# Last pair's cross-attention scores in the projection banks, ahead of and inside the output product of the pair ahead

## What is computed

```python
x = x + rwkv(layernorm(x))
# cross-attention, 16 heads of 32
q, k, v = xn @ Wq.T + bq, ctx @ Wk.T + bk, ctx @ Wv.T + bv
scores = clip(q . k / sqrt(32), -50, 50)      # masked keys: -50
probs = softmax(scores)
delta = 0.05 * ((probs . v) @ Wo.T + bo)
x = x + layernorm(delta) * gamma + beta
# feed-forward, 512 -> 2048 -> 512, ternary weights, 8-bit activations
h = gelu(bitlinear(x, w1, b1))
x = x + bitlinear(h, w2, b2)
```

## Time and profile before

| | before |
|---|---|
| median of 3 runs | 876.15 us (875.24 to 876.9) |
| profiled execution, its own time | 875.0 us |
| span of its instructions | 873.2 us |
| granted TensorE clock, mean | 0.98 |
| TensorE busy | 827.3 us (95%) |
| VectorE busy | 738.1 us (85%) |
| ScalarE busy | 505.0 us (58%) |
| GpSimd busy | 139.1 us (16%) |
| share of the chain that ended last | TensorE 72%, VectorE 16%, issue 5%, GpSimd 4% |

### The profile page before, as it was taken

How to read it: one execution, slowest core, us unless ns; L and a number is a source line. 1 busy time by engine, 2 the same in 40 slices (tenths; PEclk the granted TensorE clock), 3 DMA queues, 4 the chain that set the end, 5 groups by cost and what they waited for, 6 DMA issues and landing times.

```text
span 873.2 us, 23820 instructions
## 1 busy us (share of the span) xinstructions
PE 827.3 (95%) x10117; PEld 666.5 (76%) x10134; DVE 738.1 (85%) x1206; ACT 505.0 (58%) x728; POOL 139.1 (16%) x197
## 2 busy tenths in 40 slices
PE   7898999999999999999889999999999978999997
PEld 6798988888898888889777788888888845444453
DVE  5987989899898989986575689889888979999995
ACT  5566372846546374643535436435444457999995
POOL 1001020100102010100102000000000123676441
PEclk9899999999999999999879999999999989999999
DMA  8330112030211202023140340430232120242311
GB/s 256 126 110 19 44 34 90 15 110 15 69 44 50 75 14 86 15 86 108 65 170 2 146 162 8 146 144 29 115 144 97 39 98 25 87 143 98 109 67 55
DMA packets 36553, 72.41 MB, mean 83 GB/s; under 512 B 6081, under 2 KB 6977, under 8 KB 35433
## 3 DMA queue, kind: packets, MB, share of 16 engines
q1 hardware_dynamic: 35912, 68.93, 23.9%
q0 software_dynamic: 544, 2.10, 0.6%
HBM read 58.39 MB, written 12.58 MB: 81 GB/s over the span
## 4 chain that ended last, share of the span: by engine, by line
PE 72%; DVE 16%; issue 5%; POOL 4%; ACT 1%; DMA 1%; DVEq 0%; POOLq 0%; SPq 0%; ACTq 0%
PE P L62 11%; PE P L63 9%; PE P L64 9%; PE S L750 6%; PE S L2290 5%; PE P L2276 4%; POOL sm L378 3%; DVE xf L1026 3%; DVE E L1862 2%; PE S L636 2%; PE S L1723 2%; PE S L62 2%; PE S L63 2%; PE S L64 2%; PE S L1710 2%
## 5 line engine op out<-in xcount | busy, mean ns | idle before, releaser
L378 POOL TENSOR_TENSOR sm<-sm,mhalf 128x16 f32<-128x16 f32 x8 | 30.6, 3828 | 303.7 <-DVE sm L1121 303.7
L2290 PE MATMUL S<-wq,hqT 128*128 128x512 bf16 x255 | 59.9, 380 | 2.6 <-ACT hqT L2214 2.2
L750 PE MATMUL S<-R,K 64*64 64x32 f32 x3072 | 57.2, 223 | 2.8 <-DVE K L1072 1.7
L750 PEld LDWEIGHTS S<-R,K 64*64 64x64 f32 x3072 | 51.5, 137 | 10.4 <-issue 4.7
L2276 PE MATMUL P<-wq,xqT 128*128 128x512 bf16 x240 | 56.1, 387 | 2.3 <-ACT xqT L2192 1.2
L1862 DVE TENSOR_SCALAR E<-S,upper 128x2048 f32<-128x2048 f32 x16 | 37.6, 2349 | 24.2 <-PE S L1710 24.0
L1536 ACT ACTIVATE E<-E 128x2048 f32<-128x2048 f32 x16 | 30.6, 1913 | 45.3 <-DVE E L1862 45.3
L1868 DVE RECIPROCAL rec<-S 128x512 f32<-128x512 f32 x16 | 53.6, 3350 | 1.8 <-PE S L1725 1.8
L1026 DVE TENSOR_TENSOR xf<-P,xx 128x1024 f32<-128x1024 f32 x40 | 48.7, 1218 | 7.3 <-PE P L657 7.2
L1033 DVE TENSOR_TENSOR xf<-xf,xnT 128x1024 f32<-128x1024 f32 x40 | 49.1, 1227 | 1.1
L2276 PEld LDWEIGHTS P<-wq,xqT 128*128 128x128 bf16 x256 | 24.7, 100 | 29.3 <-issue 2.7
(11 more groups left out here) (300 smaller groups left out, 2701.0 us busy)
## 6 DMA issues: line engine op xcount, KB each, us to landing
wch<-in_wff SPq DMA_DIRECT2D x32, 256.0 KB, 3.1
cwch<-in_wff SPq DMA_DIRECT2D x8, 1024.0 KB, 7.0
xt<-in_x SPq DMA_DIRECT2D x8, 512.0 KB, 4.5
y<-in_x SPq DMA_DIRECT2D x8, 512.0 KB, 3.6
out<-y SPq DMA_DIRECT2D x8, 512.0 KB, 3.3
cxt<-out SPq DMA_DIRECT2D x8, 512.0 KB, 4.1
ct<-in_ctx SPq DMA_DIRECT2D x8, 512.0 KB, 5.1
cxr<-out SPq DMA_DIRECT2D x8, 512.0 KB, 7.0
```

Of the source, the lines that this page charges most:

```text
L378: pool.tensor_tensor(sm[:, 2, :], sm[:, 1, :], mhalf[:, 0:2 * H], ALU.pow).then_inc(y_rstd, 1)
L750: mm = pe.matmul(ps[half_rows(side), par, b, k, :], K[head_rows(par), r % 2, at:at + HALF], right_tokens(par, g, side, i), start=True, sto ...
L2290: mm = pe.matmul(O[:, :], hqT[b % 2][:, k, :], w2q[:, k, :], start=k == 0, stop=k == NF - 1)
```

## The change

The last pair's scores no longer go through `scores` and `clip`. The first set is written to P[2], P[3], S[2] and S[3] before `project_out(6)`, which needs only S[0] and S[1]. The second set is written to the four banks of P between the two halves of `project_out(6)`, as soon as VectorE has clipped the half of the first set that lay in P. VectorE clips the first set in two halves inside its last regular step, ahead of pair 5's `add_last`, and the second set ahead of the feed-forward block's first front. The hand-written lists that follow are reordered on TensorE, ScalarE and VectorE: both `weigh` come before product 0, `project_out(7)` comes before turn 1 and product 1, and ScalarE's `high_out(7)` comes behind GELU 0 and its `center`, VectorE's `low(7)` ahead of front 1. GpSimd's and SyncE's lists stay as they are.

```diff
--- before.py
+++ after.py
@@ -1338,7 +1338,7 @@
     shd = sb("shd", [P, 2])
     shf = sb("shf", [P, 2])
     ident, mhalf = persist["ident"], persist["mhalf"]
-    PFa, PFb, S = psum["X0"], psum["X1"], psum["S"]
+    PFa, PFb, F, S = psum["X0"], psum["X1"], psum["F"], psum["S"]
 
     wload = {n: sem(f"wload_{n}") for n in "qkvo"}
     wsplit_hi = sem("wsplit_hi")
@@ -1357,6 +1357,7 @@
     v_ready = sem("v_ready")
     scores_done = sem("scores_done")
     clipped = sem("clipped")
+    first_clipped = sem("first_clipped")
     exps = sem("exps")
     pv_done = sem("pv_done")
     rec_ready = sem("rec_ready")
@@ -1618,20 +1619,20 @@
         def finish(f):
             last = PAIRS - 1
             run_to_last(act, step)
+            attend(last, 0)
             copy_delta(last - 1)
+            attend(last, 1)
             f["copy_x"](0)
-            attend(last, 0)
-            attend(last, 1)
+            f["gelu"](0)
+            f["center"](0)
+            high_out(last)
+            f["square"](0)
             normalize_delta(last - 1)
-            f["gelu"](0)
             f["copy_x"](1)
-            f["center"](0)
-            f["square"](0)
-            high_out(last)
+            copy_delta(last, d_last)
             f["gelu"](1)
             f["center"](1)
             f["square"](1)
-            copy_delta(last, d_last)
             f["copy_x"](2)
             f["copy_h"](0)
             f["step"](4)
@@ -1682,7 +1683,7 @@
                 mm = pe.matmul(ps, os_[1][:, k, T * b:T * b + T], W["o"][0][:, k, :], start=False, stop=k == NC - 1)
             return mm
 
-        def project_out(r):
+        def project_out(r, between=None):
             if isinstance(r, int) and r == 0:
                 pe.wait_ge(wsplit_lo, 4)
                 pe.wait_ge(bias_lo, 2)
@@ -1693,7 +1694,28 @@
                 if b == 0:
                     pe.wait_ge(ol_ready, r + 1)
                 mm = out_low(S[:, b, :], b)
+                if b == 0 and between is not None:
+                    between()
             mm.then_inc(out_done, 1)
+
+        def score_banks(banks, b):
+            for k in range(NC):
+                for j in range(4):
+                    rows = slice(XD * j, XD * j + XD)
+                    mm = pe.matmul(banks[j][:, T * k:T * k + T], K[rows, k, T * b:T * b + T], Q[rows, k, T * b:T * b + T],
+                                   start=True, stop=True)
+            mm.then_inc(scores_done, 1)
+
+        def last_scores_first():
+            pe.wait_ge(q_ready, NC * PAIRS)
+            pe.wait_ge(k_ready, NC * PAIRS)
+            pe.wait_ge(o_ready, 2 * (PAIRS - 1))
+            score_banks([F[:, 2, :], F[:, 3, :], S[:, 2, :], S[:, 3, :]], 0)
+
+        def last_scores_second():
+            pe.wait_ge(v_ready, PAIRS)
+            pe.wait_ge(first_clipped, 1)
+            score_banks([F[:, j, :] for j in range(4)], 1)
 
         def scores(q, b):
 
@@ -1804,19 +1826,17 @@
         def finish(f):
             last = PAIRS - 1
             run_to_last(pe, step)
-            project_out(last - 1)
-            scores(last, 0)
-            pe.wait_ge(k_ready, NC * PAIRS)
-            pe.wait_ge(v_ready, PAIRS)
+            last_scores_first()
+            project_out(last - 1, last_scores_second)
+            pe.wait_ge(delta, last)
+            weigh(last, 0)
             f["turn_x"](0)
-            scores(last, 1)
+            weigh(last, 1)
             pe.wait_ge(ternary, PAIRS)
             f["product"](0)
-            weigh(last, 0)
-            weigh(last, 1)
+            project_out(last)
             f["turn_x"](1)
             f["product"](1)
-            project_out(last)
             pe.wait_ge(o_ready, 2 * PAIRS)
             f["turn_x"](2)
             pe.wait_ge(delta, PAIRS)
@@ -1861,6 +1881,21 @@
                     dve.wait_ge(pv_done, 2 * q)
             dve.tensor_scalar(E[b][:, :, :, :].rearrange("p j k t -> p (j k t)"), S[:, :, :].rearrange("p j n -> p (j n)"),
                                              upper[:, bass.ds(q * 2 + b, 1)], -LIMIT, ALU.min, ALU.max).then_inc(clipped, 1)
+
+        def clip_last_first():
+            q = PAIRS - 1
+            dve.wait_ge(scores_done, 2 * q + 1)
+            dve.wait_ge(pv_done, 2 * q)
+            dve.tensor_scalar(E[0][:, 0:2, :, :].rearrange("p j k t -> p (j k t)"), F[:, 2:4, :].rearrange("p j n -> p (j n)"),
+                              upper[:, 2 * q:2 * q + 1], -LIMIT, ALU.min, ALU.max).then_inc(first_clipped, 1)
+            dve.tensor_scalar(E[0][:, 2:4, :, :].rearrange("p j k t -> p (j k t)"), S[:, 2:4, :].rearrange("p j n -> p (j n)"),
+                              upper[:, 2 * q:2 * q + 1], -LIMIT, ALU.min, ALU.max).then_inc(clipped, 1)
+
+        def clip_last_second():
+            q = PAIRS - 1
+            dve.wait_ge(scores_done, 2 * q + 2)
+            dve.tensor_scalar(E[1][:, :, :, :].rearrange("p j k t -> p (j k t)"), F[:, :, :].rearrange("p j n -> p (j n)"),
+                              upper[:, 2 * q + 1:2 * q + 2], -LIMIT, ALU.min, ALU.max).then_inc(clipped, 1)
 
         def attended(q, b):
 
@@ -1954,6 +1989,8 @@
                 low(q, os_, o[:, :, :, :].rearrange("p k b t -> p (k b t)"), oh_ready, ol_ready)
                 if first:
                     quantize(1)
+            if isinstance(q, int) and q == PAIRS - 2:
+                clip_last_first()
             if r is not None:
                 add_last(r)
 
@@ -1989,17 +2026,16 @@
             last = PAIRS - 1
             run_to_last(dve, step)
             f["open"]()
+            clip_last_second()
             f["step"](0)
-            clip(last, 0)
+            attended(last, 0)
+            attended(last, 1)
             last_stats(last - 1)
-            clip(last, 1)
+            low(last, os_, o[:, :, :, :].rearrange("p k b t -> p (k b t)"), oh_ready, ol_ready)
             last_norm(last - 1)
             f["step"](1)
-            attended(last, 0)
-            attended(last, 1)
             f["middle_variance"](0)
             f["middle"](0)
-            low(last, os_, o[:, :, :, :].rearrange("p k b t -> p (k b t)"), oh_ready, ol_ready)
             f["middle_scale"](0)
             f["front"](2)
             f["step"](3)
```

## The result

| | before | changed |
|---|---|---|
| median, measured side by side | 875.69 us (4 runs, 874.18 to 876.90) | 885.46 us (4 runs, 884.56 to 886.62) |
| profiled execution, its own time | 875.0 us | 886.62 us |
| span of its instructions | 873.2 us | 884.8 us |
| granted TensorE clock, mean | 0.98 | 0.977 |

The changed kernel takes 1.0113 [1.0091, 1.0135] of the time before. It is **slower by 9.8 us**. The forecast was slower by 6.1.

The account below looks back on a forecast made before the run. The start of the gapless feed-forward steps, the first `xo` at 744.05, was taken to bound the kernel. GELU 1's 7.6 us delay, partly returned, plus a second dip made it 6.1 late: 876.15 + 6.1 = 882.3 us, range 878.8 to 885.7.

Parts of the forecast that it names:

- Steps 1 to 3: Seam start: early scores, clips ahead of the first normalization, then product 0 until 714.6; GELU 0 at 714.7, 1.2 us gained.
- Step 4: Last output product: `coh` at 719.0, TensorE idle 5.5 us, product charged 7.85 us at the dipped clock, ending at 728.0.
- Step 5: Product 1 behind the last output product: starts at 729.5 instead of 719.80, GELU 1 at 733.3, 7.6 us late.
- Step 6: Product 2: starts at 740.8 instead of 735.94, 4.8 us late, 2.8 of the 7.6 being returned.
- Step 7: First VectorE `output` (`xo`): 4.4 us late at full clock, 6.1 us late, at 750.2, with a second clock dip.
- The second dip: Half clock on product 2 after TensorE idles 4.8 us, charged 1.71 us (5.11 against 3.40).
- The 129.15 us behind the first `xo`: Feed-forward steps from the first `xo` to the end, taken as untouched by the change.
- the first dip: Half clock in the last output product after TensorE's 5.5 us idle; charged 7.85 us against 6.12 at full clock.
- longer dips: Rival, 12%: each clock dip lasts 6.8 us instead of 3.4, losing at most 1.7 each; up to 885.7 us.
- faster: Rival, 4%: removing VectorE's waits of 1.65 and 1.60 brings the first `xo` forward by 3.2 us; 872.9 us.
- full clock: Rival, 10%: scores and weighings keep TensorE busy, both dips (1.73 and 1.71) fall away; 878.8 us.
- No difference: Rival, 5%: slack behind takes up the 4 to 6 us, or the rearrangement hides and costs nothing; 876.2 us.

Follow-up runs that it names:

- The second run: The changed kernel with turn 1, product 1 and what feeds them ahead of the last output product again; 882.85 us, ratio 1.0077.
- the first experiment: The changed kernel with its early scores and clips kept, but everything behind them in the order of before on three engines; 878.95 us, ratio 1.0030.
- e2: Same kernel as the second run: the changed kernel with product 1 and its feeding lists ahead of the last output product; 882.85 us, ratio 1.0077.
- e3: The changed kernel with ScalarE making `coh` ahead of GELU 0 instead of behind its centering; 883.15 us, ratio 1.0085.
- e4: The changed kernel with overwritten matmuls filling TensorE's gaps, 22 ahead of the last output product and 24 ahead of product 2; 881.51 us, ratio 1.0074.
- the best lists: The first experiment's kernel with the last clip behind the first normalization, first weighing ahead of product 0, and VectorE's `middle` ahead of `middle_variance`; 874.90 us, ratio 1.0001.

## Why the prediction was right or wrong

**Right:** the side, the chain that makes the time, and its place. Slower had a chance of 0.91. The time, 885.46, is 3.2 us above the forecast and only 0.24 below the top of the range; the repeat, 885.87, lies just above it. That top was worked out for two dips of 6.8 us; the dips were shorter, and the 1.5 us behind the seam, which nothing in the prediction stands for, helped to carry the time up to it. That the number fell inside is partly luck. Of the signs named, GELU 2 at 744 to 746 and the first `xo` at 748 to 750 were missed: by before's time they came at 748.1 and 751.9. Step by step:

- Steps 1 to 3, scores, clips, first product. Product 0 was forecast at +15.35 and came at +15.55, at full clock. A half clip costs half a clip, as I took it. The table load hides behind product 0: ScalarE issued it at 712.45, right behind its last copy, and the GELU began at 717.37, as the product ended. GELU 0 gained 0.82 us, not 1.2. Of a table switch, the Trainium skill (ScalarE: Activation LUTs, What ACT_TABLE_LOAD costs) says that it takes about 1.28 us of load and 1.38 of drain, 2.66 together. The trace agrees with the first figure only. In the kernel before the GELU starts 1.30 us after the load, so no drain of that size is in the path; the measurement decides.
- Step 4, `coh` and the last output product. `coh` came 0.34 late, TensorE's idle time was 5.38 for 5.5. The product's own term was mis-sized: charged 7.85, **measured 8.82**, since it stood at half clock for 5.6 us (722.70 to about 728.3), where the row that set the price did for 3.5.
- Step 5, product 1 behind it. This is the step that costs, as said: GELU 1 is 8.87 us late, forecast 7.6. Of the 1.24 more, 0.97 are step 4's. The step takes it that product 1's operands are there when the output product ends, and never looks. VectorE's list, with `low` and so `coh` ahead of the second normalization, gave them at +30.91, 1.5 us ahead of the forecast turn at +32.45. That it held is luck, and the run with `coh` ahead of GELU 0 shows it failing. The second run and the one with the copy moved bear out the mechanism, with one addition: the sentence that the copy of the last `d` "is hidden behind product 1" holds in the changed kernel but not once product 1 is moved, where it costs 4.7 us at the first `xo`.
- Step 6, product 2: 5.75 us late, forecast 4.8. The excess is that of GELU 1, less 0.3.
- Step 7, first `xo`: 7.83 late, forecast 6.1. The second dip was charged 1.71. Product 2 until its bias took 743.96 to 749.88, 5.92, against 732.82 to 736.36, 3.54, for product 1 at full clock: **2.38**. The price of 1.71 was taken from a product 0 that stood at half clock only from 709.16 to 712.6, 3.4 of its 5.11 us; product 2 did from 743.96 to about 748.8, 4.8 us. The row of a product's 3.40 also holds only 15 of its 16 matmuls; to the bias, all 16 take 3.54.
- The 129.15 us behind the first `xo`, "that the change doesn't touch". This **failed**, by 1.50 us, and it is the term that I had no line for. One interval between two `xo` is 9.28 instead of 8.90. And at the end a wait of about 2 us on TensorE is followed by half clock in one kernel and not in another. TensorE's timeline, first of the changed kernel:

```profile
871.04 5.31 PE L2326 MATMUL S<-wq,hqT 128*128 128x512 bf16 x16 [1.97 <-ACT hqT L2250]
```

Of the kernel before:

```profile
860.81 3.40 PE L2290 MATMUL S<-wq,hqT 128*128 128x512 bf16 x15 [2.20 <-ACT hqT L2214]
```

And of the first experiment:

```profile
864.22 3.63 PE L2327 MATMUL S<-wq,hqT 128*128 128x512 bf16 x16 [1.97 <-ACT hqT L2251]
```

All three are the same product at the same place, the last but one. The changed kernel and the first experiment wait the same 1.97 us; one then runs at half clock and the other at full. The runs with a profile fall into two groups, 130.65 to 130.76 us behind the first `xo` (the change, its repeat, e2, e3, e4) and 129.14 to 129.57 (before and all the others). What sorts them wasn't tested.

The sum, then: 6.1 forecast; 1.0 more for the first dip, 0.7 more for the second, 1.5 behind the seam. That is 9.3, and the medians differ by 9.8. The rival "longer dips" named the right cause for the seam's excess, and its price of up to 1.7 a dip covers both; it was given 12%, and says nothing of the 1.5 us behind the seam. The rival "faster" wanted the last output product to start by about 715 in before's time; it started at 720.4. Whether 715 is the point wasn't tested: with `coh` ahead of GELU 0 it started at 717.05, and the result was slower than before all the same. The rival "full clock" is refuted by the windows. "No difference" fell too, but what stood for it came true by itself: the Trainium skill (TensorE: Matmul & The Clock Gate, HAM oscillation — how this bites in real kernels) reports for another matmul kernel that PSUM double-buffering gave no further gain, and with the lists mended the runs here agree: 874.90 and 876.02 us with the early scores, against 875.36 and 875.83.

## What to carry to other kernels

When a list is rewritten by hand, look at each engine for the first instruction that waits for another engine, and list all that stands behind it. Then ask, for what stands behind, whether its own operands would have been there: here TensorE's product 1 stood behind a product that waited for `coh`, and so did VectorE's normalization that feeds it, so TensorE's list alone shows only part. The next GELU, once product 1 was early, stood behind a copy that waited. Undoing the first order on all its lists gave back 3 of the 10 us, undoing both gave back all. Taking waits away by a buffer was worth little here: the best lists took VectorE's marked waits in the seam from 4.5 to 3.4 us, and no median shows it.

## What was not expected of the hardware

- The same wait of 1.97 us on TensorE, in the same place (the last product but one), was followed by 1.2 GHz in one kernel (5.31 us for 16 matmuls) and by 2.4 GHz in another (3.63). Waits of 2.29 us and 2.07 us were followed by half clock, one of 2.20 us by full. So a dip can't be read off the length of the gap alone. The Trainium skill (TensorE: Matmul & The Clock Gate, Part 1: The HAM clock gate) says that the gate runs free of the program and that the cold stretch changes with its phase from run to run. These rows agree in that equal gaps end differently; the repeat of the change, with its dips in the same places, shows little of such a change between two runs of one kernel.
- Filling gaps with matmuls whose results are overwritten moved a dip instead of removing it in the kernel before: product 1 took 5.30 us, where at full clock its 16 matmuls take 3.61.
